# A gated cross-attention and a quantized feed-forward layer: row sums from a column of ones in v, probabilities turned in halves, normalizations in halves

## The reference

```python
x = x + tanh(g_xattn[0]) * xattn(layernorm(x), ctx_4096, Wq, bq, Wk, bk, Wv, bv, Wo, bo)
x = x + tanh(g_ffn[0]) * ffn(layernorm(x), ...)            # 1024 -> 3584 -> 1024
def xattn(x, cond, ...):                                   # B, C, T = 16, 128, 1024
    q, k, v = Wq @ x + bq, Wk @ cond + bk, Wv @ cond + bv
    k, v = pad(k, 8, 7), pad(v, 8, 7)                      # along T
    k_win, v_win = windows of 16 of k and v                # B, 8, 16, T, 16
    dots = einsum('bhdt,bhdtw->bhtw', q, k_win) * 16 ** -0.5
    out = einsum('bhtw,bhdtw->bhdt', softmax(dots), v_win)
    return Wo @ out + bo
def ffn(x, ...):
    return (silu(x @ gate) * (x @ up)) @ down              # each weight (int - zero) * scale
```

## Time and profile before

| | |
|---|---|
| median of 3 runs | 1,631.78 us |
| lowest, highest | 1,631.67, 1,643.83 us |
| the profiled execution | 1,639.15 us |
| its span | 1,636.9 us |
| TensorE busy | 1,556.0 us, 95% |
| VectorE busy | 1,450.1 us, 89% |
| ScalarE busy | 1,054.3 us, 64% |
| GpSimd busy | 1,256.5 us, 77% |

### The profile page before, as it was taken

One profiled execution on the slowest core, in us unless ns is written; L12 is line 12 of the kernel. 1 busy time (PEld: TensorE's weight loads), 2 busy tenths in 40 slices (PEclk: granted clock), 3 DMA queues, 4 the chain that ended last, 5 costly groups with the idle time before them and its releaser, 6 DMA issues.

```text
span 1636.9 us, 40533 instructions
## 1 busy us (share of the span) xinstructions
PE 1556.0 (95%) x16614; PEld 811.9 (50%) x16614; DVE 1450.1 (89%) x1425; ACT 1054.3 (64%) x1191; POOL 1256.5 (77%) x925
## 2 busy tenths in 40 slices
PE   5899999898789999999999999999999999999996
PEld 3566666666434444444444444444444444444444
DVE  4688877777598999999999999999999999999997
ACT  4577777777566666666666666666666666666652
POOL 4576776666546888888888888888888888888865
PEclk9899999999899999999999999999999999999999
DMA  4666665645434666666666666676666676667569
GB/s 121 161 149 147 172 150 139 156 125 140 128 117 114 148 152 153 152 153 152 152 152 155 154 154 155 153 154 147 153 152 153 146 155 156 151 154 155 116 180 321
DMA packets 192274, 249.50 MB, mean 152 GB/s; under 512 B 14446, under 2 KB 138030, under 8 KB 192074
## 3 DMA queue, kind: packets, MB, share of 16 engines
q1 hardware_dynamic: 168186, 163.74, 35.3%
q0 software_dynamic: 22752, 82.85, 28.8%
q10 hardware_dynamic: 1152, 0.33, 0.1%
HBM read 113.92 MB, written 16.78 MB: 80 GB/s over the span
## 4 chain that ended last, share of the span: by engine, by line
PE 90%; issue 4%; SPq 2%; POOL 1%; DVE 1%; DMA 1%; ACT 1%; ACTq 0%; DVEq 0%; POOLq 0%
PE bank L1182 69%; PE bank L1091 3%; PE bank L1080 3%; PE bank L1123 2%; PE bank L1043 2%; PE bank L1054 2%; PE bank L1039 2%; PE bank L1047 2%; PE bank L1101 1%; PE bank L1070 1%; PE bank L1051 1%; PE bank L1059 1%; POOL oacc L620 1%; SPq L396 1%; DMA gates<-in_g_ffn_dram 1%
## 5 line engine op out<-in xcount | busy, mean ns | idle before, releaser
L969 DVE SCALAR_TENSOR_TENSOR acc<-bank,scale,acc 128x1024 f32<-128x1024 f32 x784 | 969.6, 1279 | 52.0 <-PE bank L1182 15.1
L1182 PE MATMUL bank<-xT,w_int 128*128 128x512 f16 x3584 | 846.4, 379 | 7.5 <-DVE xT L920 3.7
L620 POOL TENSOR_TENSOR oacc<-oacc,d_part 128x1024 f32<-128x1024 f32 x219 | 536.7, 2455 | 54.0 <-ACT d_part L806 48.7
L1182 PEld LDWEIGHTS bank<-xT,w_int 128*128 128x128 f16 x3584 | 349.9, 98 | 431.6 <-DVE xT L920 5.3
L806 ACT ACTIVATE d_part<-bank,scale 128x1024 f32<-128x1024 f32 x219 | 244.1, 1115 | 200.9 <-PE bank L1182 197.0
L1182 PE MATMUL bank<-h_hi,d_int 128*128 128x512 f16 x896 | 339.6, 379 | 2.1 <-ACT d_part L806 1.8
L1182 PE MATMUL bank<-h_lo,d_int 128*128 128x512 f16 x896 | 339.6, 379 | 0.0
L806 ACT ACTIVATE d_more<-bank,scale 128x1024 f32<-128x1024 f32 x158 | 176.3, 1116 | 154.5 <-PE bank L1182 154.5
L564 POOL TENSOR_TENSOR raw_z<-raw_w,raw_z 128x512 int32<-128x512 int32 x168 | 225.6, 1343 | 19.1 <-DMA raw_z<-in_L_ffn_gate_z_dram 11.1
L622 POOL DMA_DIRECT2D oacc<-d_more x158 | 150.2, 951 | 114.1 <-ACT d_more L806 107.8
L610 POOL TENSOR_TENSOR h_lo<-acc,h_hi 128x1024 f16<-128x1024 f32 x56 | 129.5, 2312 | 23.1 <-ACT h_hi L788 23.1
(11 more groups left out here) (86 smaller groups left out, 1530.1 us busy)
## 6 DMA issues: line engine op xcount, KB each, us to landing
oacc<-d_more POOLq DMA_DIRECT2D x158, 512.0 KB, 5.2
raw_w<-in_L_ffn_gate_w_dram SPq DMA_DIRECT2D x56, 256.0 KB, 3.4
raw_z<-in_L_ffn_gate_z_dram SPq DMA_DIRECT2D x56, 256.0 KB, 4.2
raw_w<-in_L_ffn_up_w_dram SPq DMA_DIRECT2D x56, 256.0 KB, 3.4
raw_z<-in_L_ffn_up_z_dram SPq DMA_DIRECT2D x56, 256.0 KB, 4.0
raw_w<-in_L_ffn_down_w_dram SPq DMA_DIRECT2D x56, 256.0 KB, 2.9
raw_z<-in_L_ffn_down_z_dram SPq DMA_DIRECT2D x56, 256.0 KB, 3.7
vt<-vn_hl SPq DMA_DIRECT2D x64, 192.0 KB
```

Of the source, the lines that this page charges most:

```text
L620: nc.gpsimd.tensor_tensor(into, into, d_part[:, (n - 1) % 2, :], ALU.add).then_inc(d_added, 1)
L969: nc.vector.scalar_tensor_tensor(out=into, in0=pair[u % 4][:, :, :].rearrange("p h r -> p (h r)"), scalar=scale[:, par, i, m, k:k + 1], in ...
L1182: last = nc.tensor.matmul(dst[:, h, :], weights, rows_of(h, part), start=(part == 0), stop=(part == 1))
```

## The change

- `vt` and `vn_hl` get a 33rd column of ones for each head, so the mix gives the row sums too. `add_up` and its matmuls go. The mixed values take two banks (64 columns for each head, of which 33 are used), and the reciprocal moves into `take_mix`, ahead of the reduction.
- The probabilities are turned in halves of 8 transposes through one bank: half 0 of step `n - 1` at the end of step `n`, half 1 of step `n - 2` after the first projection. `take_pT` takes one half each. The mix moves behind all three projections of the step.
- The projections go k, v, q over steps 0, 1 and 2 of a batch, which were k, q, v; in step 3 `x` comes last.
- `moments` go in halves over the steps: those of x of the next batch in steps 0 and 1, those of the finished row in steps 1 and 2. `norm_x` goes in two halves at the end of step 1, and q waits for its own half. `oT` has a tile of its own (it shared `xn`'s).
- `set_residual` goes in halves behind the splits of steps 0 and 3.
- The mask matmuls contract over 64 rows rather than 128, one on the upper and one on the lower half of the array.
- SyncE loads the x rows behind the placing of v. In the prologue ScalarE waits for the gates later, issues half of the first moves of k itself, and TensorE waits for the masks behind the first projections.

```diff
-        proj, score, mixed = (bank[0], bank[1], bank[7]), bank[2:4], bank[6]
-        turned = [half[:, :].bitcast(fp16) for half in bank[4:6]]
+        proj, score, mixed = (bank[0], bank[1], bank[4]), bank[2:4], bank[6:8]
+        turned = bank[5][:, :].bitcast(fp16)
...
-            return ((x_end, k[:1], k[1:]), (q[:1], q[1:], t[:1]), (v[:1], v[1:], t[1:]), (x, o[:1], o[1:]))[s]
+            return ((x_end, k[:1], k[1:]), (v[:1], v[1:], t[:1]), (q[:1], q[1:], t[1:]), (o[:1], o[1:], x))[s]
...
                 if b + 2 < B:
-                    load_x(b + 2)
                     load_ctx(b + 2)
                 if b + 1 < B:
                     place_v(b + 1)
+                if b + 2 < B:
+                    load_x(b + 2)
...
             def norm_x(b):
                 act.wait_ge(shift_done, b + 1)
                 if b:
-                    act.wait_ge(projected, done("o", b - 3, 1) if b >= 3 else done("q", b - 1, 1))
-                nc.scalar.activation(xn[:, :], rows[b % 4][:, :], ACT.Identity, bias=shift[:, 0:1], scale=rstd[:, 0:1])\
-                    .then_inc(x_normed, 1)
+                    act.wait_ge(projected, done("q", b - 1, 1))
+                for n, normed in enumerate((half_normed, x_normed)):
+                    half = slice(n * HALF, (n + 1) * HALF)
+                    nc.scalar.activation(xn[:, half], rows[b % 4][:, half], ACT.Identity,
+                                         bias=shift[:, 0:1], scale=rstd[:, 0:1]).then_inc(normed, 1)
...
-            act.wait_ge(gates_loaded, 32)
-            nc.scalar.activation(tanh_g[:, :], gates[:, :], ACT.Tanh).then_inc(gates_ready, 1)
             norm_x(0)
             act.wait_ge(bias_loaded, 48)
-            for t in first_tasks[:4]:
+            for t in first_tasks[:2]:
+                take_high(*t)
+
+            act.wait_ge(emptied_proj, low_done("k", 0, 1))
+            act.wait_ge(km_zeroed[0], 1)
+            for h in range(HG):
+                lo = GC + HD * h
+                act.dma_start(km[0][lo:lo + HD, :, h, PAD:PAD + T], k_hl[lo:lo + HD, :, :]).then_inc(k_moved, 16)
+            for t in first_tasks[2:4]:
                 take_high(*t)
...
-            def take_pT(n):
-                act.wait_ge(probs_turned, n + 1)
-                for hg in range(2):
-                    last = nc.scalar.activation(pT[0:2 * KW, n % 2, hg, :], turned[hg][0:2 * KW, :], ACT.Copy)
-                last.then_inc(pT_ready, 1)
+            def take_pT(n, hg):
+
+                act.wait_ge(probs_turned, 2 * n + hg + 1)
+                nc.scalar.activation(pT[0:2 * KW, n % 2, hg, :], turned[0:2 * KW, :], ACT.Copy).then_inc(pT_ready, 1)
...
-                nc.vector.tensor_reduce(o_sum[:, n % 2], all_mixed.rearrange("p x a d -> p x d a"), AX.X, ALU.add)\
-                    .then_inc(mix_taken, 1)
+                nc.vector.reciprocal(rinv[:, n % 2], all_mixed[:, :, 2 * HD]).then_inc(sums_inverted, 1)
+                nc.vector.tensor_reduce(o_sum[:, n % 2], all_mixed[:, :, 0:2 * HD].rearrange("p x (a d) -> p x d a", a=2),
+                                        AX.X, ALU.add).then_inc(mix_taken, 1)
...
                     n = S * b + s
                     soften(b, s)
+                    if s == 1 and 0 < b < B - 1:
+                        moments_x(b + 1, (1,))
+                    if s == 2 and b >= 2:
+                        moments_row(b - 2, (1,))
                     first, second, third = tasks_of(b, s)
-                    for t in first:
+                    for t in first + second:
                         take_low(*t)
                     if n >= 2:
                         take_mix(n - 2)
-                    for t in second + third:
+                    for t in third:
                         take_low(*t)
...
-                    nc.tensor.matmul(score[hg][:, 0:JQ * KW].rearrange("p (x k) -> p x k", k=KW), spread[:, :],
-                                     window[:, :].unsqueeze(1).to_broadcast([P, JQ, KW]),
+                    r = slice(GC * hg, GC * hg + GC)
+                    nc.tensor.matmul(score[hg][:, 0:JQ * KW].rearrange("p (x k) -> p x k", k=KW), spread[r, :],
+                                     window[r, :].unsqueeze(1).to_broadcast([GC, JQ, KW]),
                                      start=True, stop=False, skip_group_check=True)
...
-                    if n >= 3:
-                        add_up(n - 3)
                     scores(b, s)
+                    if n == 0:
+                        turn_scales()
                     first, second, third = tasks_of(b, s)
-                    for t in first + second:
+                    for t in first:
+                        project(*t)
+                    if n >= 2:
+                        turn_probs(n - 2, 1)
+                    for t in second + third:
                         project(*t)
                     if n >= 2:
                         mix(n - 2)
-                    for t in third:
-                        project(*t)
                     if n == 1:
                         pe.wait_ge(s_kept, 2)
                     if n:
-                        turn_probs(n - 1)
+                        turn_probs(n - 1, 0)
```

255 lines of the change are left out of this document (122 added, 133 removed).

## The result

The changed kernel takes 1,623.3 us (median of 7 runs, 1,620.9 to 1,626.5), the kernel before on the same chip 1,633.1 (7 runs): ratio 0.994, 95% interval 0.991 to 0.997. That is 9.8 us less, where I had forecast 21; the time lies inside the range. Two later measurements of the same kernel gave 0.9945 (0.991 to 0.998) and 0.996 (0.994 to 0.998).

A forecast was written before the change was run, and what follows sets the result against it. TensorE's queue was taken to set the time. Steady batches -11, prologue -5 and last batch -5 sum to -21 us, moving the median from 1,631.8 to 1,611; range 1,588 to 1,630.

The forecast's parts named there:

- The steady sum: Attention's 14 steady batches: all terms there together give -0.8 us a batch, -11 us in all.
- Instructions of TensorE: Steady batches: row sums -1.55, wider mix +0.07, masks -0.55, order of matmuls on TensorE +0.12 us a batch.
- The masks' term: Mask matmuls over 64 rows overlap in the two array halves: -0.55 us a batch, bounds nothing to 0.70.
- masks alone: Rival, so worded though the masks don't overlap: the 33rd column is all that is gained, +8, 1,619 us; chance 0.12.
- The wait of q at the half of xn: TensorE's first q projection, step 2, waits for ScalarE's half of xn: 0.7 us a batch, counted +0.6, bounds 0 and 1.3.
- Blocks: TensorE's waits for its next 256 instructions: 2.4 us a batch in place of 1.9, +0.5; bounds -0.8 and +2.5.
- The pause in the scores of step 1: Sign: a short block of 2.0 us needs about 3.1 for the next, a sure pause of 1.1 us a batch.
- blocks pause in each batch: Rival: all five block boundaries pause 1.1 to 1.6 us, +4.1 us a batch, +57 us, 1,668; chance 0.08.
- The prologue's term: Start to first steady batch: k whole earlier, half its moves on ScalarE's queue; -5 us, bounds -8 and -1.
- The last part's term: Last batch and hand-over: the load of raw_z starts about 6 us earlier, GpSimd's wait goes; -5 us, bounds -9 and +2.
- What is late next is GpSimd's own work: Last batch: once the wait at the first raw_z is gone, GpSimd's own work is late next; no size given.
- Reciprocal, residual, turns through one bank, feed-forward part: VectorE's reciprocal, GpSimd's residual halves, turns in halves, and the unchanged feed-forward instructions: each priced at nothing.

The follow-up runs named there:

- before's three profiles: The kernel before, unchanged, profiled three times; from step 4 to step 60 they take 349.6, 344.5 and 344.3 us, mean 346.1.
- the four of after: Profiles of the changed kernel, three unchanged and one with 256 filler instructions ahead of the first scores; steady stretch 340.2 us in the mean against 346.1 before.
- all seven profiles: Profiles of the changed kernel and variants with the same code up to step 4; step 4 comes at 44.8 to 52.4 us, 49.5 in the mean.
- all nine profiles: Profiles of the changed kernel and variants with the same code in the last part, which takes 32.6 to 37.9 us, 35.1 in the mean.
- phase64: Changed kernel plus 32 one-column matmuls (64 instructions) ahead of the first scores, moving every block boundary; 1,647.3 us, ratio 1.007 to the kernel before.
- phase160: Changed kernel plus 80 one-column matmuls (160 instructions) ahead of the first scores, moving every block boundary; 1,657.9 us, ratio 1.013 to the kernel before.

## Why the prediction was wrong by half

Point by point, with the means above. The steady sum was -11 us and is -5.9:

- Instructions of TensorE. I had -1.55 + 0.07 - 0.55 + 0.12 = -1.91 us a batch. With pauses, waits and half the half clock taken off, before's three profiles leave 312.4, 312.8 and 312.2 us, the four of after 293.2, 291.5, 293.2 and 293.5: -19.6, or -1.40 a batch, so 7 us less than counted. **The masks' term failed**: 0.16 a batch for 0.55, 5.5 us in all. In the chain the pair takes 0.27 for 0.35 us. I took the overlap from the small score tiles; between the two mask matmuls there is little, and the rival "masks alone" was right in this. The remaining 1.6 us aren't assigned.
- The wait of q at the half of xn: 0.65 for 0.6 to 0.7, right. All of TensorE's waits together rose by 6.6 us; I had 8.4. They are 8.5 us in the mean now, and before's 1.9 are the one wait at step 4 that the change was to take away with the prologue.
- Blocks: +6.9 us of pauses over 14 batches for +7. The size is right. The pause in the scores of step 1 is there (10.3 and 14.6 us over 12 batches in two profiles, 0.9 and 1.2 for 1.1). The reason was half of one: I priced the short block alone. The fetch starts behind the boundary, late where v's moves and ctx are in the queues, which makes the others late too, and at other places of the boundaries much later. The rival "blocks pause in each batch", with 8 in 100, was closer than it looks: its price, a third to a half of the 57 us counted there, came with 64 or 160 instructions more.
- The granted clock was in no term, and none was missing: 14.2 us at half clock before, 14.7 after, +0.3 us of work.
- Together -19.6 + 6.6 + 6.9 + 0.3 = -5.8, and -5.9 was measured.

**The prologue's term failed**: -1.8 for -5 (-2.0 with all seven profiles). Scores came at 21.3, not 18. What was missed is on the chain:

```profile
3.13 8.84 DMA row<-in_x_dram
11.99 1.30 DVE stats L874 x2
13.31 0.21 DVE mv L878
13.52 1.28 DVE k_hl L932 x2
14.82 0.73 ACTq L734
...
30.88 3.88 DMA vt<-vn_hl
```

VectorE takes the moments of batch 1 ahead of the low half of k, and these wait for a row block of 512 KB that lands at 11.97; k's moves begin at 14.8 and not at 13.5. Then the take of the next v waits until 34.84 for the copies of the first, with xn and q behind it on ScalarE, and block pauses take what is left.

**The last part's term may have been too large**: -3.5 for -5, or -4.3 with all nine profiles. The wait of 3.69 us at the first raw_z is down to 0.75, as said, but GpSimd's normalizations now stand behind its takes of raw_z and the splits, and TensorE waits for them twice:

```profile
399.88 1.27 POOL raw_z L564
401.15 0.59 POOL xT L557
401.74 0.14 issue
401.87 1.09 PE bank L1070 x4
```

"What is late next is GpSimd's own work" stood in the prediction without a price. Taking that wait away gave back almost nothing, so it isn't the whole cause. What goes with the length of this part is the half clock in it: of the nine profiles the four with 3.4 us of it take 32.6 to 34.7 us, the two with 6.8 take 34.9 and 36.5, the three with 13.7 take 36.3 to 37.9. Before has 13.7, 13.7 and 18.8. No run set it on purpose, so it stays a candidate. Reciprocal, residual, turns through one bank, feed-forward part: priced at nothing, and nothing is seen of them.

So of the 10 us that the profiles miss of the 21, about 7 are instructions, 5.5 of these the masks, 3 the prologue and 1 to 1.5 the last part, with 2 given back where waits were fewer than counted. The range held the time because it was wide, 42 us; the forecast moved by twice what was measured.

## What to carry to other kernels

Where an engine's own instruction stream is the bound, a pause in it is a race between two things that both can be read off: how long the block in hand runs, and how far behind the boundary the fetch of the next starts, which was later here where v's moves and ctx were under way. Cutting instructions or waits shortens the block that hides the fetch, so part of such a gain comes back as a pause; and if a loop's body is near a multiple of the block, adding a few instructions anywhere ahead of it moves every boundary and can change the time by more than the edit under study. Check that with a filler of a whole block and of parts of one before a gain or loss of 1 or 2% is put down to an edit, and profile the kernel before more than once, since one long execution here made 6 us of gain look like 11.

## What the runs showed of the hardware

- The fetch of TensorE's next 16 KB of instructions starts 0 to 6.6 us behind a block boundary, takes 0.9 to 1.8 us where TensorE then stands, and TensorE resumes about 1.4 us behind its end. In empty queues it starts 0.8 to 1.6 us behind the boundary, with v's moves and ctx in them 2.9 to 5.2 us; with the row's load or store under way it came after 0.2 to 0.6 us in six batches. The Trainium skill (Runtime: NRT & Kernel Launch, Instruction fetch mechanics) calls crossing a boundary mostly hidden; here 23 to 26 us of 344 to 350 stand at boundaries in the kernel before and 28 to 54 of 336 to 384 in the others, and the measurement decides.
- Shifting all boundaries by 64 or 160 instructions cost 20 and 31 us, by 256 nothing.
- Pauses of 2 to 3 us in each batch (phase64, phase160) went with 56 and 57 us at a granted clock of 0.5 in the steady stretch, the changed kernel's pauses of about 1 us with 9 to 24.
- Two mask matmuls of 64 rows in the two halves of the array took 0.27 us where two of 128 rows took 0.35, and the time of the kernel does not tell the two apart.
